# Convolution, attention and expert kernel: row maxima placed in 16 marked rows by one ScalarE copy, scores one head further ahead, steps of head, tail, ranks and taps reordered

## The chip, the cores and the metric

The kernel runs on one core of a Trainium2 chip. The metric is device time in microseconds (us); less is better. The engines are TensorE (PE; PEld is its weight load), VectorE (DVE), ScalarE (ACT), GpSimd (POOL) and SyncE (SP), each with its own instruction stream, tied together by semaphores.

## What is computed

```python
x = x + conv3x3(relu(norm(image_attention(conv3x3(x)))))   # 16 images, 128 channels, 16 x 16 pixels
t = tokens(x)                                              # 16 x 256 tokens of 128
z = layernorm(t)
sim = (z @ wq_s / 4) . (z @ wk_s)       # 8 heads of 16, within one image: 256 x 256 per head
retrieved = softmax(sim) @ (z @ wv_r)   # 2 value sets of 16
gate = softmax((z @ wq_r / 4) . (retrieved @ wk_ret))      # over the 2 sets
t = t + (gate . retrieved) @ w_out
z = layernorm(t)
t = t + sum over the best 2 of 8 experts: share * (silu(z @ W1[e]) @ W2[e])
```

## The kernel before

Three parts follow each other: the image attention with its convolutions (to about 142 us), the token stage (`token_attention`, to about 497), and the experts on rows scattered by expert (`experts`). The change is all in `token_attention`.

Tokens are in 8 chunks (g) of 512, two images each (b = 0, 1; image 2g + b); `body(g, ring, stage)` is one chunk on each engine, `last_body` the last. The stages are FIRST (g = 0), MIDDLE (1 to 5), LAST_BUT_ONE (6) and LAST (7). A body has two halves, one per image, of eight steps s, one per head. The order in each engine's stream is written out by hand; each engine works its own list in order, and a waiting instruction holds all that is behind it.

Per head, TensorE computes the scores of the *next* image (`scores`, L1596, banks ps_s), VectorE takes their row maxima (`row_max`, L1280). After eight heads VectorE negates and splits them into a high and a low part (`split_max`, L1289 to L1293), TensorE turns them (`turn_max`, L1605), and VectorE and ScalarE place two head pairs each into rows 96 to 99 of `q_stack` (`place_max`, L1298 and L1053). Rows 96 to 99 of `k_stack` hold ones and zeros that pick a head of a pair. So the second product, `shifted_scores` (L1617, 100 rows), gives transposed scores less their maximum. ScalarE takes the exponential (`exponent`, L1059), TensorE multiplies it with the values (`retrieve`, L1632, per pair of heads) and turns the result (`turn_ret`, L1641); ScalarE copies in between (`keep_pair`, `keep_ret`). TensorE's shifted scores of an image wait for `max_placed`.

Beside these run the other chunks' parts. *Head* of chunk g + 2: nine convolution taps (`conv_taps`, in MIDDLE stages by LATE_TAPS and behind step 7), `add_conv` on VectorE, `head_turn`, `keep_t` on ScalarE (L1024), `norm_stats` on VectorE (L1248 to L1256), `rstd` on GpSimd (a pow, L937), `normalise` on VectorE (L1262), `head_turn_back`, `split_zt`, `low_zt`, then `head_k`, and in the next body `head_q` and `head_tokens`. k and q of a chunk go to DRAM and come back stacked by head (SyncE's `stack`: `bounce` L890, `fill_k` L899, `fill_q` L905). *Tail* of chunk g - 1: `retrieve` parts 0 to 2 on VectorE (sum of a product of L1313, a gate whose exponential is ScalarE's L1083, o_tok L1334), `tail_turn` (L1655), `tail_out`, `add_attention`, statistics, `rstd`, `normalise_t2` on VectorE, `copy_rows` on GpSimd (L963), `tail_turn_back`, `tail_route`. *Ranks* of chunk g - 2: `route` parts 0 to 2 on VectorE, `share_exp` on ScalarE, `rank` on TensorE, `place` on VectorE, and GpSimd's `scatter` (eight indirect DMAs, L973).

Banks: ps_conv holds taps, z_tok's turn, k, and the tail's routing; ps_x holds the maxima's turn in most stages, t_chunk's turn, q, o_tok and the ranks; tokens use both.

## Time and profile before

| | us |
|---|---|
| runs | 684.0, 685.08, 688.95 |
| median | 685.08 |
| profiled execution, its own time | 685.38 |
| span of the profiled execution | 683.6 |
| TensorE busy in the span | 566.0 |
| VectorE busy | 475.9 |
| ScalarE busy | 333.1 |
| GpSimd busy | 262.6 |

The span runs from the first to the last instruction on the core. Busy times are sums over the whole span; what an edit in one stage is worth is read from the waits and the order of that stage.

### The profile page before, as it was taken

How to read it: one execution, taken by the hardware profiler on the slowest of the kernel's cores; microseconds unless marked ns; L12 is line 12 of the kernel's file. 1: busy time of each engine (PE TensorE's matmuls, PEld its weight loads, DVE VectorE, ACT ScalarE, POOL GpSimd, SP SyncE). 2: the span in 40 equal slices, each digit the busy share in tenths (PEclk: the TensorE clock that was granted, in tenths of full speed). 3: DMA queues.
4: the chain of work that ended last, by engine and by line, in shares of the span. 5: the costliest groups of instructions: out<-in, count | busy, mean ns of one | idle time of the engine just before them, and what ended most of it. 6: DMA issues, size and time to landing. Idle time of an engine off the chain costs nothing. (4 is left out here: it accounts for less than half of the span.)

```text
span 683.6 us, 10705 instructions
## 1 busy us (share of the span) xinstructions
PE 566.0 (83%) x3180; PEld 439.7 (64%) x3180; DVE 475.9 (70%) x1227; ACT 333.1 (49%) x718; POOL 262.6 (38%) x328
## 2 busy tenths in 40 slices
PE   5999999849788988979898887876169999999910
PEld 4888888636565767666666665654058888888810
DVE  6886774855557777777878778785537767767715
ACT  3322302233356465554636355544148888888800
POOL 3245443458000100141413314247603666666660
PEclk9999999959879999999999999998569999999965
DMA  7994145649531405041230505001278777776109
GB/s 262 365 347 145 57 170 185 203 164 372 153 116 39 155 1 155 1 151 36 96 92 31 157 3 184 9 25 48 76 251 293 234 243 230 246 235 221 51 6 363
DMA packets 55224, 105.46 MB, mean 154 GB/s; under 512 B 8744, under 2 KB 21689, under 8 KB 55040
## 3 DMA queue, kind: packets, MB, share of 16 engines
q1 hardware_dynamic: 50176, 96.24, 42.6%
q0 software_dynamic: 4992, 8.54, 3.6%
q8 instruction: 26, 0.43, 0.3%
q14 instruction: 30, 0.25, 0.1%
HBM read 58.15 MB, written 48.42 MB: 156 GB/s over the span
## 5 line engine op out<-in xcount | busy, mean ns | idle before, releaser
L1949 POOL DMA_INDIRECT y_slots<-virt,pad_l x92 | 95.7, 1041 | 72.5 <-DVE virt L2001 49.5
L1280 DVE TENSOR_REDUCE s_max<-bank 128x2 f32<-128x512 f32 x128 | 87.4, 689 | 40.3 <-PE bank L1596 39.8
L1059 ACT ACTIVATE s_expd<-bank 128x512 f32<-128x512 f32 x128 | 76.9, 602 | 53.5 <-PE bank L1617 52.3
L973 POOL DMA_INDIRECT x_slots<-rows,slot_of x64 | 63.1, 986 | 55.9 <-DVE rows L1408 38.3
L937 POOL TENSOR_TENSOR ln_rstd<-ln_var,power 128x4 f32<-128x4 f32 x17 | 17.4, 1026 | 173.4 <-DVE ln_var L1256 173.4
L1989 DVE TENSOR_TENSOR k_stack<-virt,k_stack 128x512 fp32r<-128x512 f32 x92 | 63.4, 689 | 24.9 <-ACT k_stack L1968 24.2
L1632 PE MATMUL bank<-s_expd,rvx 128*64 128x256 f32 x512 | 70.5, 397 | 1.5 <-ACT s_expd L1059 1.0
L61 PE MATMUL bank<-pad_h,u_h 128*128 128x512 f32 x144 | 59.9, 416 | 8.4 <-DVE pad_l L399 8.4
L1617 PE MATMUL bank<-q_stack,k_stack 100*128 100x256 f32 x256 | 61.8, 325 | 5.0 <-DVE q_stack L1298 5.0
L1968 ACT ACTIVATE k_stack<-virt 128x512 fp32r<-128x512 f32 x92 | 58.2, 633 | 10.1 <-PE bank L63 7.2
L1963 ACT ACTIVATE virt<-bank 128x512 f32<-128x512 f32 x92 | 55.0, 597 | 14.3 <-PE bank L63 13.9
L1596 PE MATMUL bank<-k_stack,q_stack 96*128 96x256 f32 x256 | 55.5, 303 | 3.9 <-DMA q_stack<-qk_rows 2.3
L63 PE MATMUL bank<-pad_h,u_l 128*128 128x512 f32 x144 | 58.0, 403 | 0.0
L62 PE MATMUL bank<-pad_l,u_h 128*128 128x512 f32 x144 | 57.9, 402 | 0.0
L1617 PEld LDWEIGHTS bank<-q_stack,k_stack 100*128 100x128 f32 x256 | 43.0, 199 | 18.0 <-DVE q_stack L1298 7.0
L1596 PEld LDWEIGHTS bank<-k_stack,q_stack 96*128 96x128 f32 x256 | 42.5, 204 | 6.2 <-DVE s_max L1280 2.8
L1632 PEld LDWEIGHTS bank<-s_expd,rvx 128*64 128x64 f32 x512 | 31.5, 138 | 22.6 <-ACT s_expd L1059 5.1
L1066 ACT ACTIVATE ret_f<-bank 128x256 f32<-128x256 f32 x64 | 24.4, 382 | 39.8 <-PE bank L1632 39.8
L61 PE MATMUL bank<-k_stack,pad_h 128*128 128x512 f32 x92 | 40.5, 440 | 0.0
L1984 DVE TENSOR_TENSOR k_stack<-bank,k_stack 128x512 fp32r<-128x512 f32 x23 | 15.9, 692 | 30.5 <-ACT k_stack L1958 30.5
L61 PEld LDWEIGHTS bank<-pad_h,u_h 128*128 128x128 f32 x144 | 27.8, 193 | 14.3 <-issue 8.3
L62 PE MATMUL bank<-k_stack,pad_h 128*128 128x512 f32 x92 | 36.7, 399 | 0.0
(260 smaller groups left out, 1321.8 us busy)
## 6 DMA issues: line engine op xcount, KB each, us to landing
x_slots<-blank SPq DMA_DIRECT2D x8, 2112.0 KB, 17.3
pad_h<-w_split SPq DMA_DIRECT2D x23, 512.0 KB, 4.4
q_stack<-w_split SPq DMA_DIRECT2D x23, 512.0 KB, 5.7
qk_rows<-qk SPq DMA_DIRECT2D x16, 512.0 KB, 3.0
k_stack<-qk_rows SPq DMA_DIRECT2D x96, 64.0 KB, 2.4
q_stack<-qk_rows SPq DMA_DIRECT2D x48, 128.0 KB, 2.6
pad_l<-x_slots SPq DMA_DIRECT2D x23, 264.0 KB, 5.2
e_raw<-in_w SPq DMA_DIRECT2D x16, 256.0 KB, 3.0
```

The lines of the kernel that those rows point to most:

```text
L61: pe.matmul(out, w_h, x_h, start=start, stop=False)
L62: pe.matmul(out, w_h, x_l, start=False, stop=False)
L63: return pe.matmul(out, w_l, x_h, start=False, stop=stop)
L973: pool.indirect_dma_start(out=x_slots[:, :], out_offset=bass.IndirectOffsetOnAxis(ap=slot_of[:, ring, k, j:j + 1], axis=0), in_=rows[:, ri ...
L1059: nc.scalar.activation(expd[:, s % 4].rearrange("p a i -> p (a i)"), ps_st[s % 2][:, :], ACT.Exp).then_inc(exp_done, 1)
L1280: nc.vector.tensor_reduce(s_max[:, :, s], ps_s[s % 2][:, :].rearrange("p (a j) -> p a j", a=2), AX.X, ALU.max).then_inc(max_done, 1)
L1596: last = pe.matmul(ps_s[s % 2][:, i * PIX:(i + 1) * PIX], q_stack[0:96, ring, s // 2, at + i * P:at + (i + 1) * P], k_stack[0:96, ring, s, ...
L1617: last = pe.matmul(ps_st[s % 2][:, i * PIX:(i + 1) * PIX], k_stack[0:100, ring, s, at + i * P:at + (i + 1) * P], q_stack[0:100, ring, s // ...
L1632: last = pe.matmul(ps_pv[p % 2][h * RF:(h + 1) * RF, 0:PIX], rvx[:, ring, 2 * b + a, :], expd[:, 2 * (p % 2) + h, a, :], start=(a == 0), s ...
L1949: pool.indirect_dma_start(out=y_slots[:, :], out_offset=bass.IndirectOffsetOnAxis(ap=ids, axis=0), in_=y_rows[:, t % 2, j, :], in_offset=N ...
L1968: nc.scalar.activation(hid_h[:, f], hid[:, f], ACT.Copy).then_inc(hid_high, 1)
L1989: nc.vector.tensor_tensor(hid_l[:, f], hid[:, f], f32(hid_h[:, f]), ALU.subtract).then_inc(hid_ready, 1)
```

## The change

Each image's maxima go to 16 rows (96 to 111) of all pairs of `q_stack` by one ScalarE copy that reads the turned maxima four times; the same 16 rows of `k_stack` mark, per head, its two rows with ones (`mark_heads`, two GpSimd copies in place of 24 memsets). VectorE's `place_max` is gone. Shifted scores use 112 rows. The turned maxima stay in one of the two score banks, no more in ps_x or ps_conv. `ahead_of` moves scores and row maxima one head on: at step s those of head s + 1 of the next image, at step 7 head 0 of the one after. `turn_max` stands at step 7. `head_q` of chunk g + 2 is issued at the end of body g (in FIRST also the old one at step 0). Tokens go to step 2, the tail's output to 6, its turn back to 5, its routing to 6, ranks to step 0 of the second half in ps_conv, the head's turn back to 5, taps to 3, 5, 6 and 7. The tail's normalise of chunks 0 to 5 moves from VectorE to GpSimd (`tail_rows`), its statistics to the second half, and VectorE's statistics wait for z_ready of the norm before (L1251's place). At the start four banks serve the first image's scores, `fill_q` of chunk 0 goes over ScalarE's DMA queue, and the low parts of images 12 to 15 come later. Lines left out are shown as "..."; where the lines of before are left out, they stand in the kernel above.

```diff
-    LATE_TAPS = {4: range(0, 2), 5: range(2, 3), 6: range(3, 4), 7: range(4, 6)}
+    LATE_TAPS = {3: range(0, 2), 5: range(2, 5), 6: range(5, 6), 7: range(6, 8)}
...
     def route_bank(u):
-        return ps_s[1] if u == IMAGE_A else ps_conv
-    def max_bank(stage):
-        return ps_x if stage in (FIRST, MIDDLE) else ps_conv
+        return ps_s[1] if u == IMAGE_A else ps_x if u < NCH - 2 else ps_conv
...
+    def ahead_of(image, s):
+        image, s = image + 1 + (s + LEAD) // S, (s + LEAD) % S
+        return (image, s) if image < 2 * NCH else None
+    def score_bank(image, s):
+        return ps_s[(9 * image + s - (1 if s else 2)) % 2]
+    def max_bank(image):
+        return ps_s[9 * image % 2]
+    first_banks = ps_s + ps_st
...
+        def first_stack():
+            sp.wait_ge(k_ready, 1)
+            bounce(sp, 0, 0, k_bounced)
+            sp.wait_ge(k_bounced, 16)
+            fill_k(sp, 0, 0, 0)
+            fill_k(sp, 0, 0, 1)
...
-        pool.memset(f32(m_split[:, :, :, :]), 0.0).then_inc(stack_init, 1)
+        pool.tensor_tensor(head_of[:, :], ident[0:2 * S, 0:2 * S:2], ident[0:2 * S, 1:2 * S:2], ALU.add
+                           ).then_inc(heads_marked, 1)
...
+        def normalise(n, dst, g):
+            pool.wait_ge(ln_power, n + 1)
+            for j in range(G):
+                last = pool.tensor_scalar(dst[:, j, :], chunk(resid, g)[:, j * P:(j + 1) * P], ln_mv[:, j, 0:1],
+                                          ln_rstd[:, j:j + 1], ALU.subtract, ALU.mult)
+            last.then_inc(z_ready, 1)
+        def tail_rows(g, ring):
+            rstd(tail_norm(g))
+            need(pool, scattered[ring], 2 * G * 16 * (g // 2))
+            normalise(tail_norm(g), rows[:, ring, 0, :, 0:P], g)
+        def mark_heads(ring):
+            pool.tensor_copy(k_stack[MAX_AT:MAX_AT + 2 * S, ring, :, :],
+                             head_of[:, :].unsqueeze(2).broadcast_to([2 * S, S, CH])).then_inc(ones_made, 1)
+        pool.wait_ge(stack_init, 2 * S)
+        pool.wait_ge(heads_marked, 1)
+        mark_heads(0)
+        pool.wait_ge(ones_made, 1)
         rstd(0)
         pool.wait_ge(ln_power, 1)
-        for part in range(1, 2 * S, 2):
-            pool.memset(ones_rows[0:2, part], 0.0).then_inc(ones_made, 1)
-        pool.wait_ge(ones_made, 3 * S)
+        mark_heads(1)
+        pool.wait_ge(ones_made, 2)
...
-            rstd(tail_norm(g - 1))
+            if g < NCH - 1:
+                tail_rows(g - 1, (g - 1) % 2)
+            else:
+                rstd(tail_norm(g - 1))
...
-        def place_max(g, b, ring, src=ps_x):
-            act.wait_ge(m_turned, 2 * g + b + 1)
-            for p in (2, 3):
-                nc.scalar.activation(q_stack[96:100, ring, p, b * PIX:(b + 1) * PIX],
-                                     src[32 * p:32 * p + 4, 0:PIX], ACT.Copy).then_inc(m_odd, 1)
+        def place_max(image):
+            act.wait_ge(m_turned, image + 1)
+            at = image % 2 * PIX
+            wide = max_bank(image)[0:2 * S, 0:PIX].unsqueeze(1).broadcast_to([2 * S, NP, PIX])
+            nc.scalar.activation(q_stack[MAX_AT:MAX_AT + 2 * S, image // 2 % 2, :, at:at + PIX], wide, ACT.Copy
+                                 ).then_inc(m_placed, 1)
...
+                if s == 0 and stage != LAST:
+                    split_k(g + 1)
+                if s == 1 and stage != LAST:
+                    split_q(g + 1)
+                if s == 2 and stage != LAST:
+                    keep_tok(g + 1, 0, 1 - ring)
+                    keep_tok(g + 1, 1, 1 - ring)
+                if s == 2 and stage != FIRST:
+                    gate(g - 1, 1)
+                if s == 5 and stage != FIRST:
+                    keep_o(g - 1)
+            place_max(2 * g + 1)
             keep_pair(g, 0, NP - 1)
...
             for s in range(S):
                 exponent(g, 1, s)
                 if s == 0:
                     keep_ret(g, 0, NP - 1)
                 pairs_behind(g, 1, s)
...
+                if s == 0 and stage in (FIRST, MIDDLE):
                     keep_t(g + 2)
...
+                if s == 0 and g >= 2:
+                    share_exp(g - 2)
+                if s == 3:
                     gate(g, 0)
...
+                if s == 5 and stage != FIRST:
+                    keep_z2(g - 1)
+                if s == 5 and stage in (FIRST, MIDDLE):
                     split_zt(g + 2)
+                if s == 7 and stage != FIRST:
+                    keep_logits(g - 1, 1 - ring)
+            place_max(2 * g + 2)
             keep_pair(g, 1, NP - 1)
...
                     gate(g - 1, 1)
...
+                if s == 5:
                     keep_o(g - 1)
                 if s == 6:
                     share_exp(g - 2)
+            place_max(2 * g + 1)
             keep_pair(g, 0, NP - 1)
...
+        def bounce_first_q():
+            act.wait_ge(q_ready, 1)
+            bounce(act, 0, 2, q_bounced)
+        def stack_first_q():
+            act.wait_ge(q_bounced, 16)
+            act.wait_ge(stack_init, 2 * S)
+            fill_q(act, 0, 0, 0)
+            fill_q(act, 0, 0, 1)
         keep_t(0)
         split_zt(0)
         keep_t(1, ps_s[1])
         split_k(0)
         split_q(0)
         keep_tok(0, 0, 0)
+        bounce_first_q()
         keep_tok(0, 1, 0)
+        split_zt(1)
+        stack_first_q()
         image_pair(6)
...
             dve.wait_ge(ln_steps, LS * n + 1)
+            need(dve, z_ready, n)
             nc.vector.memset(ln_var[:, :], 0.0)
...
-        def row_max(g, b, s):
-            dve.wait_ge(s_done, 2 * S * g + S * b + s + 1)
...
+                                    ).then_inc(max_done, 1)
+            if s == S - 1:
+                split_max(image)
+        def row_max_ahead(image, s):
+            if at := ahead_of(image, s):
+                row_max(*at, score_bank(*at))
+        def split_max(image):
...
         def body(g, ring, stage):
             for s in range(S):
...
+                row_max_ahead(2 * g, s)
+                if s == 0 and stage != LAST:
+                    low_k(g + 1)
+                if s == 0 and stage != LAST:
+                    low_q(g + 1)
+                if s == 1 and stage != FIRST:
+                    retrieve(g - 1, 1, 0)
+                if s == 2 and stage != FIRST:
+                    retrieve(g - 1, 1, 1)
+                if s == 2 and stage == FIRST:
+                    low(12)
+                if s == 3 and stage != FIRST:
+                    retrieve(g - 1, 1, 2)
+                if s == 3 and g >= 2:
+                    route(g - 2, ring, 0)
+                if s == 3 and stage == FIRST:
+                    low(13)
+                if s == 4 and stage == FIRST:
+                    low(14)
+                if s == 5 and g >= 2:
+                    route(g - 2, ring, 1)
+                if s == 5 and stage == FIRST:
+                    low(15)
+                if s == 6 and g >= 2:
+                    route(g - 2, ring, 2)
+                if s == 6 and stage != FIRST:
+                    add_attention(g - 1)
             for s in range(S):
...
+                if s == 0 and stage == MIDDLE:
                     add_conv(g + 2)
...
+                row_max_ahead(2 * g + 1, s)
+                if s == 0 and stage != FIRST:
+                    norm_stats(tail_norm(g - 1), t2_kept, g - 1)
                 if s == 1:
                     retrieve(g, 0, 0)
+                if s == 2 and g >= 2:
+                    place(g - 2, ring, ps_conv)
+                if s == 2 and stage in (FIRST, MIDDLE):
+                    norm_stats(2 * g + 2, t_kept, g + 2)
+                if s == 4 and stage in (FIRST, MIDDLE):
+                    normalise(2 * g + 2, z_tok, g + 2)
                 if s == 4:
                     retrieve(g, 0, 1)
                 if s == 5:
                     retrieve(g, 0, 2)
...
+                if s == 7 and stage in (FIRST, MIDDLE):
+                    low_zt(g + 2)
         def last_body():
             g, ring = NCH - 1, 1
             for s in range(S):
...
+                row_max_ahead(2 * g, s)
                 if s in (1, 2, 3):
                     retrieve(g - 1, 1, s - 1)
...
+                if s in (4, 5, 6):
+                    route(g - 2, ring, s - 4)
+            add_attention(g - 1)
+            norm_stats(tail_norm(g - 1), t2_kept, g - 1)
+            place(g - 2, ring, ps_conv)
             normalise_t2(g - 1, 0)
...
         normalise(1, z_tok, 1)
...
         low_zt(1)
...
+        add_conv(2, ps_pv[0])
         for s in range(S):
...
+            row_max(0, s, first_banks[s % 4])
+        for s in range(LEAD):
+            row_max(1, s, score_bank(1, s))
...
-                if dst is ps_conv:
-                    need(pe, tok_copied, 4 * g)
...
+        def scores(image, s, bank):
+            g, b = image // 2, image % 2
             if s == 0:
                 pe.wait_ge(stacked[b], STACK * (g + 1))
...
             at = b * PIX
             for i in range(2):
...
+                last = pe.matmul(bank[:, i * PIX:(i + 1) * PIX],
+                                 q_stack[0:96, g % 2, s // 2, at + i * P:at + (i + 1) * P],
+                                 k_stack[0:96, g % 2, s, at:at + PIX], start=True, stop=True)
             last.then_inc(s_done, 1)
...
+        def scores_in_turn(image, s):
+            if s == 0:
+                pe.wait_ge(max_done, S * image - 1)
+            elif s == 2:
+                pe.wait_ge(m_placed, image)
+            else:
+                pe.wait_ge(max_done, S * image + max(s - 1, 1))
+            scores(image, s, score_bank(image, s))
+        def scores_ahead(image, s):
+            if at := ahead_of(image, s):
+                scores_in_turn(*at)
+        def turn_max(image):
+            pe.wait_ge(m_steps, 3 * image + 3)
             for i in range(2):
...
+                src = f32(m_split[:, i].rearrange("p s c -> p (s c)"))
+                last = pe.transpose(max_bank(image)[0:2 * S, i * P:(i + 1) * P], src, ident[:, :])
             last.then_inc(m_turned, 1)
...
-                                 k_stack[0:100, ring, s, at + i * P:at + (i + 1) * P],
-                                 q_stack[0:100, ring, s // 2, at:at + PIX], start=True, stop=True)
+                                 k_stack[0:112, ring, s, at + i * P:at + (i + 1) * P],
+                                 q_stack[0:112, ring, s // 2, at:at + PIX], start=True, stop=True)
...
             max_placed(2 * g)
             for s in range(S):
                 shifted_scores(g, 0, s, ring)
...
+                scores_ahead(2 * g, s)
                 pairs_behind(g, 0, s, ring)
...
+                if s == 7:
+                    turn_max(2 * g + 1)
+                if stage == FIRST and s == 0:
+                    head_q(g + 1)
+                if s == 2 and stage != LAST:
+                    head_tokens(g + 1)
+                if s == 4 and stage != FIRST:
+                    need(pe, tok_copied, 4 * g + 6)
+                    tail_turn(g - 1)
+                if s == 6 and stage != FIRST:
+                    tail_out(g - 1)
                 if stage == MIDDLE and s in LATE_TAPS:
+                    if 0 in LATE_TAPS[s]:
+                        need(pe, tok_copied, 4 * g + 8)
                     conv_taps(g + 2, LATE_TAPS[s])
+            if stage == MIDDLE:
+                conv_taps(g + 2, range(8, 9))
             retrieve(g, 0, NP - 1, ring)
...
             max_placed(2 * g + 1)
             for s in range(S):
                 shifted_scores(g, 1, s, ring)
...
+                scores_ahead(2 * g + 1, s)
                 pairs_behind(g, 1, s, ring)
...
+                if s == 7:
+                    turn_max(2 * g + 2)
+                if s == 0 and g >= 2:
+                    if ahead:
+                        need(pe, t_ready, g + 3)
+                    else:
+                        need(pe, tok_copied, 4 * g + 8)
+                    rank(g - 2, ps_conv)
+                if s == 1 and ahead:
+                    need(pe, t2_kept, g + 0)
                     head_turn(g + 2)
...
+                if s == 5 and stage != FIRST:
+                    if ahead:
+                        need(pe, t_kept, g + 3)
+                    else:
+                        need(pe, t2_kept, g + 0)
+                    tail_turn_back(g - 1, 1 - ring)
+                if s == 5 and ahead:
+                    need(pe, spot_read, 4 * g - 7)
                     head_turn_back(g + 2, 2 * g + 3)
...
+                if s == 6 and stage != FIRST:
+                    tail_route(g - 1)
             retrieve(g, 1, NP - 1, ring)
...
             if ahead:
+                need(pe, zt_steps, 2 * g + 5)
                 head_k(g + 2)
+            if ahead:
+                need(pe, logits_kept, g + 0)
+                head_q(g + 2)
         def last_body():
             g, ring = NCH - 1, 1
             max_placed(2 * g)
             for s in range(S):
                 shifted_scores(g, 0, s, ring)
...
+                scores_ahead(2 * g, s)
                 pairs_behind(g, 0, s, ring)
...
+                if s == S - 1:
+                    turn_max(2 * g + 1)
+                if s == 5:
                     tail_turn(g - 1)
...
+                if s == 6:
                     tail_out(g - 1)
+                if s == 7:
+                    pe.wait_ge(logits_kept, g - 1)
+                    rank(g - 2, ps_conv)
             retrieve(g, 0, NP - 1, ring)
...
-        conv_taps(2, range(4, 8), ps_pv[0])
+        conv_taps(2, range(4, 9), ps_pv[0])
         head_k(1)
         for s in range(S):
-            scores(0, 0, s, 0)
-            if s == 0:
-                conv_taps(2, range(8, 9), ps_pv[0])
-        turn_max(0, 0)
-        pe.wait_ge(ones_made, 3 * S)
+            need(pe, max_done, s - 3)
+            scores(0, s, first_banks[s % 4])
+        scores_in_turn(1, 0)
+        turn_max(0)
+        pe.wait_ge(ones_made, 2)
```

## Rows read from the trace of the kernel before

**Rows 1.** The page, part 1: busy us (share) xinstructions

```profile
PE 566.0 (83%) x3180; PEld 439.7 (64%) x3180; DVE 475.9 (70%) x1227; ACT 333.1 (49%) x718; POOL 262.6 (38%) x328
```

**Rows 2.** Windows, chunk 4's halves: length, busy by engine, PEclk, DMA share, GB/s

```profile
317.60:333.67 16.07, 13.56 (x103) 9.83 (x102) 13.26 (x44) 9.71 (x25) 2.26 (x2) 1.00 0.01 2
333.67:355.57 21.90, 20.07 (x125) 15.13 (x125) 16.54 (x54) 9.99 (x26) 8.63 (x11) 1.00 0.48 145
```

**Rows 3.** Waits of PE, 190 to 458: us in total, times, longest

```profile
PE bank L1605 <- DVE m_split L1293: 12.3, 10, 1.6
PE bank L1655 <- DVE o_tok L1334: 11.7, 7, 1.9
PE bank L1617 <- DVE q_stack L1298: 5.0, 5, 1.2
PE bank L1557 <- DVE t_chunk L1242: 3.4, 5, 0.7
```

**Rows 4.** Timeline of PE, 328 to 345: start, us, what, [idle before <- releaser]

```profile
329.56 1.08 PE L1632 MATMUL bank<-s_expd,rvx 128*64 128x256 f32 x8
332.26 0.41 PE L1605 MATMUL bank<-ident,m_split 128*128 128x128 f32 x2 [1.62 <-DVE m_split L1293]
...
333.67 0.50 PE L1617 MATMUL bank<-q_stack,k_stack 100*128 100x256 f32 x2
334.01 0.40 PE L1596 MATMUL bank<-k_stack,q_stack 96*128 96x256 f32 x2
...
342.68 0.63 PE L1655 MATMUL bank<-ident,o_tok 128*128 128x128 f32 x4 [1.83 <-DVE o_tok L1334]
```

**Rows 5.** Timelines of DVE, 317 to 334 and 333 to 356

```profile
323.50 0.86 DVE L1248 BATCH_NORM_STATS2 ln_stats<-resid 128x6 f32<-128x128 f32 x4
...
324.89 0.68 DVE L1280 TENSOR_REDUCE s_max<-bank 128x2 f32<-128x512 f32 x1
...
331.73 0.18 DVE L1291 CAST m_split<-s_neg 128x16 fp32r<-128x16 f32 x1
...
332.75 0.87 DVE L1298 CAST q_stack<-bank 4x256 fp32r<-4x256 f32 x2
...
351.10 1.11 DVE L1262 TENSOR_SCALAR rows<-resid,ln_mv,ln_rstd 128x128 f32<-128x128 f32 x4 [0.15 <-POOL ln_rstd L937]
...
352.33 0.59 DVE L1291 CAST m_split<-s_neg 128x16 fp32r<-128x16 f32 x1
```

**Rows 6.** Timeline of ACT, 317 to 334

```profile
321.83 0.38 ACT L1066 ACTIVATE ret_f<-bank 128x256 f32<-128x256 f32 x1 [0.66 <-PE bank L1632]
...
322.70 0.60 ACT L1059 ACTIVATE s_expd<-bank 128x512 f32<-128x512 f32 x1
...
324.89 0.20 ACT L1105 ACTIVATE gap_e<-gap 128x4 f32<-128x4 f32 x1
```

**Rows 7.** Timelines of POOL, 95 to 142 and 350 to 382

```profile
132.61 0.90 POOL L289 TENSOR_SCALAR list_add<-tile_rows_f,row_f 2x23 f32<-2x23 f32 x1
...
349.95 1.04 POOL L937 TENSOR_TENSOR ln_rstd<-ln_var,power 128x4 f32<-128x4 f32 x1 [7.45 <-DVE ln_var L1256]
352.28 0.61 POOL L963 COPY rows<-rows 128x512 f32<-128x512 f32 x1 [1.29 <-DVE rows L1262]
```

**Rows 8.** The start: a window; PE's and DVE's timelines, 177 to 195

```profile
181.40:195.00 13.60, 10.06 (x32) 7.74 (x33) 8.51 (x16) 1.95 (x5) 0.00 (x0) 0.51 0.18 45
...
181.41 0.60 PE L1596 MATMUL bank<-k_stack,q_stack 96*128 96x256 f32 x2 [2.34 <-DMA q_stack<-qk_rows]
...
182.05 0.69 DVE L1280 TENSOR_REDUCE s_max<-bank 128x2 f32<-128x512 f32 x1 [2.65 <-PE bank L1596]
...
188.12 1.29 DVE L1280 TENSOR_REDUCE s_max<-bank 128x2 f32<-128x512 f32 x2 [0.29 <-PE bank L1596]
```

**Rows 9.** SP's timeline, 333 to 356; DMA view, 333 to 350 (KB, us to landing)

```profile
342.35 1.34 SPq L905 DMA_DIRECT2D q_stack<-qk_rows x3
...
q_stack<-qk_rows SPq DMA_DIRECT2D x6, 128.0 KB, 2.7
```

234 lines of the change are left out of this document (40 added, 194 removed).

## The prediction

> **What bounds the kernel now.** I read the page first, then the windows by half chunk, then TensorE's waits, then the timelines of one middle chunk. The page [rows 1] shows TensorE as the busiest engine, 83% against VectorE's 70%. The windows [rows 2] show one middle chunk (g = 4) in its two halves, 21.90 and 16.07 us, together 37.97 us. TensorE is busy for 20.07 + 13.56 = 33.6 us of it, at the full clock (1.00), VectorE for 16.54 + 13.26 = 29.8 us. So TensorE is the bound wherever it is fed, and about 4.2 us per chunk are waits. The waits view of the token stage [rows 3] names them: 12.3 us in which it waited to turn the maxima (`turn_max`), 5.0 us for these maxima to be placed, 11.7 us for `o_tok` at `tail_turn`, 3.4 us for `t_chunk` at `head_turn`. Together 32.4 us. In the timeline [rows 4] each wait stands in a middle chunk: 1.62 us ahead of the maxima and 1.83 us ahead of `tail_turn`; the head's 0.7 us is the third. After the last chunk GpSimd's scatters and then the experts follow; nothing there is edited, so I let that part move as a block: what the stage gains up to the first shifted scores of the last image, the end gains.
>
> **The change part by part.** I go by the profiled execution, 685.38 us around a span of 683.6; the median of the three runs, 685.08, is 0.3 lower.
>
> *The maxima's turn and placing.* Now the scores run one head further ahead. So the last row maximum and the split come at step 6, and `turn_max` stands at step 7 behind the pair's retrieve, the tail's products, shifted scores, scores and a turn. The retrieve's 1.08 and three starts of up to 0.34 [rows 4] alone are 2.1 us of TensorE work, against a need of one row maximum, 0.69, and the split's three short steps, 0.5 to 0.9 [rows 5]: covered, if VectorE is in time. Placing was two copies on VectorE (0.87, [rows 5]) beside two on ScalarE. Now it is one ScalarE copy of 1024 columns on 16 rows. No row shows that form. Bounds: 0.60 us for 512 columns, below; four copies of 256 columns at 0.38 = 1.53, above [rows 6]. The two forms differ by 256 columns and 0.22 us, so 1024 columns come to 0.60 + 2 x 0.22 = 1.04, which I take. It lies behind one retrieve (1.0), and in middle chunks behind taps or the k and q products as well. So all 17.3 us (12.3 + 5.0) go, and what is left is at the four turns without taps or head products behind them (first chunk, both of the last but one, last): 0.35 of copy that sticks out, and 0.3 where VectorE is late: 4 x 0.65 = 2.6 back.
>
> *The tail's turn.* VectorE gets the first ranks (1.1 us of `route`) behind the third part of `retrieve` instead of ahead, and TensorE puts two taps (1.5 us) ahead of `tail_turn`. Against it, tokens (keep_tok, 1.2 us on ScalarE) now stand ahead of the gate's exponential, on which VectorE waits. Followed step by step from the first shifted scores at T = 0: low_q ends at 3.5, tokens end at 4.6, the gate at 5.5, `o_tok` at 8.1, and TensorE arrives at 8.35. The 11.7 us go. In the last two chunks, which have no taps, the turn of the last is at step 5 and also late enough; in the last but one part may stay (inside the range).
>
> *The head's turn.* The 3.4 us go, since t_chunk is made first in the half. But keep_t and share_exp now stand ahead of exponential 1 on ScalarE, and keep_t waits for `head_turn`: 0.60 + 0.20 + 0.60 + signals 0.1 = 1.5 us from its end until the retrieve may start [rows 6], of which shifted scores and scores of step 2 cover 0.65. New wait 0.85 in six chunks, 5.1.
>
> *VectorE in the second half.* It loses placing (0.87) and gains the tail's statistics (1.4, [rows 5]): 13.26 - 0.87 + 1.4 = 13.8 us. TensorE's half without its waits and with head_q in it is 16.07 - 1.62 - 0.68 + 0.73 = 14.5. Only 0.7 us of slack in a half with three fixed meetings (scores 6, z_tok's turn, turn_max). Place and the statistics in one step make VectorE late by about 1 us at scores 6: I take 0.8 in each of four chunks and 0.4 in two, 4.0.
>
> *The tail's normalise on GpSimd.* Four tensor_scalars (1.11 on VectorE) go to GpSimd, behind its pow of 1.04. No row shows this form there. Bounds: 0.28 us each (VectorE's own, 1.11 / 4 [rows 5]) to 0.90 (GpSimd's only one with an operand per partition, of 23 columns [rows 7]), and beyond if its 105 more columns cost what the copy's 512 in 0.61 do (0.13): 1.03. I take 0.4 each, near to the copy's whole 0.61 for all the rows plus four starts, 1.6 in all. Queued behind it on GpSimd are copy_rows, the head's pow and the scatter; VectorE's next statistics wait for it (z_ready), and for these the head's z_tok. At U = 0 for the half's start the tail's statistics end at 2.8, pow at 3.9, normalise at 5.5, and the wait comes at 6.9. Covered up to 3.0 us for the four. What stays is the contention: [rows 5] shows the same cast of 16 columns at 0.18 and at 0.59 us, the long one at 352.33, when GpSimd's copy [rows 7] runs from 352.28 to 352.89. A VectorE operation was held until GpSimd was done. I take 0.4 in each of five chunks, 2.0. The Trainium skill (GPSIMD Engine Reference, Key points) says that GpSimd shares its SBUF interfaces with VectorE and contends with VectorE's two-port modes and two-input operations; by that rule the trace agrees, and the products of `retrieve`, two-input operations, may be held as well, which is the rival below.
>
> *Data a head earlier.* `stack` fills q for the next chunk at T = 8.7 to 10.0 (342.35 to 343.69 for T = 333.67), and a transfer lands 2.7 us later [rows 9]: T = 12.7. Scores of that image's head 0 are now asked for at step 7. In middle chunks that is about T = 15, covered. In the last but one, which has no taps, step 7 comes at about 11.4 and q at 12.7; in the first at about 11.9. Costs 1.3 + 0.8 = 2.1, with `turn_max` queued behind.
>
> *The start.* q's first fill goes over ScalarE's queue, beside k's. TensorE waited 2.34 us for q [rows 8]; then the stretch to 195 ran at a granted clock of 0.51, the level of 1.2 GHz. The tap inside the score loop goes ahead of it, t_chunk too, and four banks let TensorE run ahead, so VectorE does its eight maxima back to back. Before, they lasted from 182.05 to 189.41 [rows 8]; eight starts 0.61 apart and a last 0.69 take 5.0, 2.4 less. The longer copy takes 0.2 back: 2.2. Bounds: 0, and 5.2 if the clock keeps the upper level because TensorE idles less (some 3 us of the 13.6). GpSimd's 25 small memsets become two copies of 4096 columns: 0.61 x 8 = 4.9 each by the copy's row, about the time of what they replace, beside taps; worth 0.
>
> Matrix products with 112 rows in place of 100 stream the same columns: 0.
>
> **The sum.** Gone: 32.4 + 2.2 = 34.6. New: 2.6 + 5.1 + 4.0 + 2.0 + 2.1 = 15.8. Net 18.8. The profiled run would be 685.4 - 18.8 = 666.6, by the median 666.3: 666.
>
> **The rivals.**
> (a) *TensorE nearly without waits.* The order by hand was made engine by engine, and my followed schedules may meet waits that a loop that has settled doesn't show. For it: 32.4 us are real idle time of the busiest engine. Half the new waits (7.9) and the clock kept at the start (3): 685.4 - 34.6 + 7.9 - 3 = 656.
> (b) *GpSimd's normalise ends too late.* Each at the 0.90 of [rows 7] with 0.13 more for columns is 1.03, four are 4.1: z_ready at U = 8.0, 1.1 late for the head's statistics, then pow and z_tok, so `head_turn_back` is 1.2 us later in five chunks: 666 + 6 = 672. For it: the only row with such an operand. Against it: that row is one instruction, of 23 columns, and the first of its kind.
> (c) *VectorE becomes the bound.* Its 0.7 us of slack in the second half isn't enough for the order of its steps, and each middle chunk gives back 3.8 us, nearly its whole gain, instead of 0.8: 666 + 5 x 3.0 = 681, no clear change. For it: 13.8 of 14.5. Against it: its first half has slack (16.54 - 1.4 - 1.11 - 0.87 = 13.2 of TensorE's 20.07 - 0.73 = 19.3).
> (d) *Slower: VectorE held by GpSimd.* Place: the second half, where GpSimd's four operations run beside retrieve, place and the statistics. Price: VectorE stands still for each whole operation, as in the cast's row, 4 x 1.03 = 4.1, and (b)'s 1.2 on top, in six chunks: 32 us, of which 2 are in the sum: 666 + 30 = 696. It decides from 20.8 / 6 = 3.5 us per chunk on, that is 0.9 per operation with all of it held. Against it: the pow of 1.04 runs beside VectorE now, and VectorE's statistics and row maxima next to it keep their times.
> (e) That it doesn't do what it says: scores a head further ahead are only asked for earlier and wait for `max_done`. Same lag of two heads in two banks as before, so no gain from the banks; only the turn of the maxima gains. It is in the sum.
>
> **How the numbers follow.** Forecast 0.56, (a) 0.15, (b) 0.11, (c) 0.10, (d) 0.08. The forecast's own range is 659 to 673 (its five new terms at 0.5 to 1.4 times). The range over all is 655 to 681: it holds (a)'s and (c)'s centres and leaves out (d) and the far sides. A measurement of this kernel tells about 1% from no change, 678.2 and 691.9. Forecast, (a) and (b) lie below 678.2, with some of the forecast and (b) leaking over: 0.80 faster. (c) and what leaks: 0.12 same. (d): 0.08.
>
> **What would show it.** Right: in the waits of TensorE the groups of `turn_max`, placing and `tail_turn` under 1 us each per chunk, middle chunks at 34.8 to 35.8 us, the retrieve behind exponential 1 waiting 0.5 to 1, one wait for q's transfer in the last but one chunk, the placing copy near 1.04, GpSimd's tensor_scalar at 0.3 to 0.6. Wrong: that tensor_scalar near 1 us, VectorE's two-input operations stretched beside it, a wait of VectorE's statistics for GpSimd, TensorE waiting 3 us per half for row maxima, or the part behind the last image's first shifted scores growing.

## The result and the profile after

The changed kernel took 682.67 us (median of 20 runs, 677.61 to 690.6), the kernel before in the same rounds 686.52 (20 runs, 683.32 to 691.4). The ratio is 0.9926, 95% interval 0.9902 to 0.995: about 0.7% faster, which is within the 1% that the prediction called no change. It is taken over the runs in the usual, faster state alone (690.6 is left out), so it isn't the quotient of the two medians, 0.994. The forecast was 666, the range 655 to 681. The profiled execution took 677.61 us around a span of 675.8, 7.8 less than before's 683.6; it was the fastest of the 20.

The page of the changed kernel, part 1 (as [rows 1]), and its windows of chunk 4's two halves (as [rows 2]; here the first half stands first):

```profile
PE 567.4 (84%) x3180; PEld 441.6 (65%) x3180; DVE 460.2 (68%) x1171; ACT 339.6 (50%) x702; POOL 276.8 (41%) x330
```

```profile
333.05:352.91 19.86, 19.42 (x122) 14.43 (x120) 13.51 (x39) 9.88 (x24) 1.76 (x2) 1.00 0.46 144
352.91:370.31 17.40, 14.34 (x107) 10.71 (x106) 13.55 (x51) 10.67 (x25) 12.17 (x16) 1.00 0.06 20
```

The first half went from 21.90 to 19.86 us and is now nearly all TensorE work (19.42). The second went the wrong way, from 16.07 to 17.40 (the 16.07 in [rows 2] is the half just ahead, chunk 3's second; chunk 4's own took 16.04), with 14.34 of TensorE work: 3.06 us of waits. The waits of TensorE, 185 to 455 us (total, times, longest), beside [rows 3]:

```profile
PE bank L1635 <- DVE s_max L1331: 8.6, 7, 1.4
PE bank L1684 <- ACT s_expd L1099: 7.5, 14, 0.8
PE bank L1596 <- DVE z_tok L1313: 3.3, 4, 0.9
PE bank L1669 <- ACT q_stack L1093: 1.8, 4, 1.2
PE bank L1658 <- DVE m_split L1347: 1.6, 2, 1.2
PE bank L1707 <- DVE o_tok L1382: 0.9, 1, 0.9
```

All four groups of [rows 3] went nearly as forecast: 1.6 us are left at `turn_max` (L1658), 1.8 at placing, 0.9 at `tail_turn` (L1707), nothing at `head_turn`. In their place stand 8.6 us for row maxima ahead of the scores (L1635), 7.5 for the exponential at the retrieve (L1684) and 3.3 for the head's normalise (L1596, `z_tok`). TensorE's timeline has one of each in the second half of a middle chunk, and 0.79 + 1.36 + 0.91 = 3.06 is the whole gap of the window:

```profile
356.30 1.08 PE L1684 MATMUL bank<-s_expd,rvx 128*64 128x256 f32 x8 [0.79 <-ACT s_expd L1099]
361.59 0.51 PE L1635 MATMUL bank<-k_stack,q_stack 96*128 96x256 f32 x2 [1.36 <-DVE s_max L1331]
363.67 0.63 PE L1596 MATMUL bank<-ident,z_tok 128*128 128x128 f32 x4 [0.91 <-DVE z_tok L1313]
```

VectorE's timeline there shows why the last two come late. It waited 2.06 us for the last tap at the end of the first half (`t_chunk`), 1.00 us for the first scores of the second (the row maximum at 353.69), and then never until the head's normalise, except once, for GpSimd:

```profile
352.01 0.69 DVE L1292 TENSOR_TENSOR t_chunk<-bank,resid 128x512 f32<-128x512 f32 x1 [2.06 <-PE bank L63]
...
354.30 0.86 DVE L1298 BATCH_NORM_STATS2 ln_stats<-resid 128x6 f32<-128x128 f32 x4
...
359.04 0.86 DVE L1298 BATCH_NORM_STATS2 ln_stats<-resid 128x6 f32<-128x128 f32 x4
360.36 0.06 DVE L1302 MEMSET ln_var<- 128x4 f32 x1 [0.46 <-POOL rows L966]
...
360.86 1.28 DVE L1331 TENSOR_REDUCE s_max<-bank 128x2 f32<-128x512 f32 x2
362.18 1.34 DVE L1313 TENSOR_SCALAR z_tok<-resid,ln_mv,ln_rstd 128x128 f32<-128x128 f32 x4
```

The first statistics (354.30 to 355.8) are the tail's, new in this half; the second are the head's. GpSimd's timeline of the stretch:

```profile
355.87 1.04 POOL L960 TENSOR_TENSOR ln_rstd<-ln_var,power 128x4 f32<-128x4 f32 x1 [20.75 <-DVE ln_var L1307]
357.09 3.14 POOL L966 TENSOR_SCALAR rows<-resid,ln_mv,ln_rstd 128x128 f32<-128x128 f32 x4 [0.18 <-POOL ln_rstd L960]
```

From first shifted scores to first shifted scores, the difference of the two profiled executions adds up like this:

| stretch | before | after | difference |
|---|---|---|---|
| to the first shifted scores | 191.95 | 192.47 | +0.5 |
| first chunk | 28.45 | 28.73 | +0.3 |
| first halves of the five middle chunks | 109.65 | 99.29 | -10.4 |
| their second halves | 79.45 | 87.02 | +7.6 |
| from there to the last image | 48.42 | 41.75 | -6.7 |
| from the last image's first shifted scores to the end of the span | 225.68 | 226.54 | +0.9 |

The first row holds two things. VectorE's last step ahead of the token stage, which no edit touches, came 1.7 us earlier in the changed kernel's execution (the first line is of the kernel before, the second of the changed one):

```profile
147.04 0.23 DVE L695 TENSOR_SCALAR norm_b<-mean_sum,gb 128x16 f32<-128x16 f32 x1
```

```profile
145.34 0.23 DVE L695 TENSOR_SCALAR norm_b<-mean_sum,gb 128x16 f32<-128x16 f32 x1
```

From there to the first shifted scores it is 44.91 us before and 47.13 after: the start itself got 2.2 us longer, and 1.7 us of the profile's 7.8 are luck.

### The profile page after: what moved, and what is told of

The parts are those of the page before. It is cut to its first block and busy times, and to the rows that moved or that the text cites. A ratio compares the mean times of both kernels' runs of the same rounds, so it can differ in the third digit from the quotient of the medians.

```text
span 675.8 us, 10656 instructions
## 1 busy us (share of the span) xinstructions
PE 567.4 (84%) x3180; PEld 441.6 (65%) x3180; DVE 460.2 (68%) x1171; ACT 339.6 (50%) x702; POOL 276.8 (41%) x330
## 3 DMA queue, kind: packets, MB, share of 16 engines
HBM read 58.15 MB, written 48.42 MB: 158 GB/s over the span
## 5 line engine op out<-in xcount | busy, mean ns | idle before, releaser
L1684 PE MATMUL bank<-s_expd,rvx 128*64 128x256 f32 x512 | 71.0, 399 | 7.5 <-ACT s_expd L1099 7.5
L1008 POOL DMA_INDIRECT x_slots<-rows,slot_of x64 | 62.7, 980 | 18.6 <-issue 18.1
L1635 PE MATMUL bank<-k_stack,q_stack 96*128 96x256 f32 x256 | 55.4, 305 | 11.1 <-DVE s_max L1331 8.6
L1669 PE MATMUL bank<-q_stack,k_stack 112*128 112x256 f32 x256 | 61.8, 325 | 1.8 <-ACT q_stack L1093 1.8
L1669 PEld LDWEIGHTS bank<-q_stack,k_stack 112*128 112x128 f32 x256 | 42.0, 197 | 16.8 <-issue 10.5
L1635 PEld LDWEIGHTS bank<-k_stack,q_stack 96*128 96x128 f32 x256 | 41.5, 202 | 14.4 <-DVE s_max L1331 10.6
L1684 PEld LDWEIGHTS bank<-s_expd,rvx 128*64 128x64 f32 x512 | 31.5, 138 | 29.4 <-ACT s_expd L1099 12.6
L61 PE MATMUL bank<-k_stack,pad_h 128*128 128x512 f32 x92 | 40.8, 443 | 0.0
L62 PE MATMUL bank<-k_stack,pad_h 128*128 128x512 f32 x92 | 37.0, 402 | 0.0
L63 PE MATMUL bank<-k_stack,pad_h 128*128 128x512 f32 x92 | 36.7, 399 | 0.0
## 6 DMA issues: line engine op xcount, KB each, us to landing
x_slots<-blank SPq DMA_DIRECT2D x8, 2112.0 KB, 17.2
```

Of the source, the lines that this page charges most:

```text
L61: pe.matmul(out, w_h, x_h, start=start, stop=False)
L62: pe.matmul(out, w_h, x_l, start=False, stop=False)
L63: return pe.matmul(out, w_l, x_h, start=False, stop=stop)
L1008: pool.indirect_dma_start(out=x_slots[:, :], out_offset=bass.IndirectOffsetOnAxis(ap=slot_of[:, ring, k, j:j + 1], axis=0), in_=rows[:, ri ...
L1635: last = pe.matmul(bank[:, i * PIX:(i + 1) * PIX], q_stack[0:96, g % 2, s // 2, at + i * P:at + (i + 1) * P], k_stack[0:96, g % 2, s, at:a ...
L1669: last = pe.matmul(ps_st[s % 2][:, i * PIX:(i + 1) * PIX], k_stack[0:112, ring, s, at + i * P:at + (i + 1) * P], q_stack[0:112, ring, s // ...
```

## The experiments

My theory after the result: what moved into the second half on VectorE, the tail's statistics above all, eats what the first half gained; and the marking copies hold VectorE at the start. Rivals: GpSimd's slow normalise, or keep_t ahead of the exponential. Each ratio is to the kernel before, with its 95% interval. Lengths of halves are read between first shifted scores. "From `norm_b`" is the time from VectorE's L695 to the first shifted scores; it leaves out what varies ahead of the stage. For comparison, the changed kernel: first shifted scores at 192.47, 47.13 from `norm_b`, the last three middle second halves 17.35, 17.40 and 17.34.

**Both marking copies ahead of the first power.**

```diff
         mark_heads(0)
-        pool.wait_ge(ones_made, 1)
-        rstd(0)
-        pool.wait_ge(ln_power, 1)
         mark_heads(1)
         pool.wait_ge(ones_made, 2)
+        rstd(0)
         rstd(1)
```

> Changed kernel with both mark_heads copies ahead of the first rstd on GpSimd. Theory (the second marking copy, 3.6 us on GpSimd from 163.96, holds VectorE's first normalise, which took 4.47 us in place of 1.77): the first normalise takes 1.1 to 1.2 us, the first shifted scores start about 2.7 us earlier (189.8 for 192.5), all later stages the same length, span about 2.7 us shorter. Rival (the long normalise has another cause, e.g. the pointer operands read while their bank is written): it stays above 3 us and nothing moves. If the marking costs GpSimd so long that rstd(0) is late, half of the gain goes.

681.35 us, ratio 0.9929 (0.99 to 0.9959). A miss on the start: first shifted scores at 193.59, 48.06 from `norm_b`. The first normalise took its 1.11 us, but the hold only moved. VectorE's timeline of the changed kernel:

```profile
154.10 4.80 DVE L1268 TENSOR_TENSOR pad_l<-virt,pad_h 128x256 fp32r<-128x256 f32 x4 [0.35 <-ACT pad_h L1044]
...
163.93 4.47 DVE L1313 TENSOR_SCALAR z_tok<-resid,ln_mv,ln_rstd 128x128 f32<-128x128 f32 x4 [1.24 <-POOL ln_rstd L960]
```

and of this one, with GpSimd's line behind it:

```profile
154.29 8.23 DVE L1266 TENSOR_TENSOR pad_l<-virt,pad_h 128x256 fp32r<-128x256 f32 x4 [0.33 <-ACT pad_h L1042]
...
167.75 1.11 DVE L1311 TENSOR_SCALAR z_tok<-resid,ln_mv,ln_rstd 128x128 f32<-128x128 f32 x4 [1.24 <-POOL ln_rstd L960]
```

```profile
154.23 7.34 POOL L977 CAST k_stack<-head_of 16x4096 fp32r<-16x4096 f32 x2
```

VectorE's four subtractions end just after the two copies (162.5 and 161.6). The copies hold whatever VectorE does beside them; a later experiment puts one where it has little to do.

**The tail's statistics at step 7 of the first half.**

```diff
                 if s == 6 and stage != FIRST:
                     add_attention(g - 1)
+                if s == 7 and stage != FIRST:
+                    norm_stats(tail_norm(g - 1), t2_kept, g - 1)
             for s in range(S):
...
-                if s == 0 and stage != FIRST:
-                    norm_stats(tail_norm(g - 1), t2_kept, g - 1)
```

> Changed kernel with the tail's statistics on VectorE at step 7 of the first half (where VectorE sat idle 2.06 us) in place of step 0 of the second. Theory (VectorE is the late engine in the second half only, because of the order): row maxima of head 4 come 1.4 us earlier and z_ready from GpSimd is there, so TensorE's waits for s_max (1.36 per chunk) and z_tok (0.9) fall to under 0.5 together; second halves of middle chunks go from 17.35 to 15.2 - 15.8, span 8 to 10 us shorter than the changed kernel. Rival (GpSimd's queue sets z_tok): the wait for s_max goes, the wait for z_tok takes over with 1.5 to 2, gain under 3 us.

668.9 us, ratio 0.9766 (0.9719 to 0.9813), span 666.9, second halves of 15.46 to 15.69 in the last four middle chunks. Windows of chunk 4, then the waits of TensorE, 190 to 445 us:

```profile
328.68:348.49 19.81, 19.37 (x123) 14.43 (x121) 14.79 (x49) 9.88 (x24) 3.07 (x4) 1.00 0.48 144
348.49:364.15 15.66, 14.10 (x107) 10.70 (x106) 12.13 (x41) 10.57 (x25) 10.82 (x15) 1.00 0.07 23
```

```profile
PE bank L1684 <- ACT s_expd L1099: 7.4, 14, 0.8
PE bank L1596 <- DVE z_tok L1313: 2.9, 4, 0.8
...
PE bank L1635 <- DVE s_max L1331: 1.2, 2, 1.0
```

VectorE has 1.4 us less in the second half (12.13 for 13.55), the half is 1.74 shorter, and the first half pays nothing for it: it had that idle time. The wait for row maxima falls from 8.6 to 1.2; the one for `z_tok` stays (2.9 for 3.3), which wasn't expected. GpSimd's normalise starts earlier too, so this run alone doesn't clear it; a later one does.

**keep_t and share_exp behind exponential 1.**

```diff
-                if s == 0 and stage in (FIRST, MIDDLE):
+                if s == 1 and stage in (FIRST, MIDDLE):
                     keep_t(g + 2)
-                if s == 0 and g >= 2:
+                if s == 1 and g >= 2:
                     share_exp(g - 2)
```

> Changed kernel with keep_t and share_exp on ScalarE at step 1 (behind exponential 1) in place of step 0. Theory: the retrieve's wait of 0.8 behind exponential 1 goes in six chunks. But in middle chunks VectorE's lateness at scores 6 is a fixed meeting that this doesn't move, so TensorE only arrives earlier and waits there: the wait for s_max grows from 1.36 to about 2.1, span 0 to 1.5 us shorter. Rival (waits add up): 4 to 5 us shorter.

690.52 us, ratio 1.0051 (1.0016 to 1.0086): half a per cent slower than before. The waits, 190 to 458:

```profile
PE bank L1635 <- DVE s_max L1331: 11.7, 12, 1.4
PE bank L1596 <- DVE z_tok L1313: 4.9, 6, 0.9
PE bank L1635 <- DMA q_stack<-qk_rows: 2.5, 1, 2.5
PE bank L1684 <- ACT s_expd L1099: 1.9, 6, 0.3
```

The wait for the exponential went from 7.5 to 1.9 us and came back at the row maxima and `z_tok`: two second halves took 17.36 and 17.39, as before the edit. Three others took 18.58, 21.44 and 21.65, at a granted clock of 0.91, 0.76 and 0.76. Windows through the last of these:

```profile
360.86:365.00 4.14, 4.14 (x38) 3.43 (x36) 3.25 (x15) 3.37 (x9) 1.04 (x1) 1.00 0.00 0
365.00:370.00 5.00, 3.05 (x22) 1.96 (x20) 4.40 (x21) 2.29 (x6) 4.89 (x8) 1.00 0.00 0
370.00:374.00 4.00, 3.08 (x19) 2.46 (x19) 3.78 (x12) 2.10 (x5) 3.20 (x4) 0.59 0.12 37
374.00:378.00 4.00, 4.00 (x20) 3.05 (x17) 0.85 (x4) 0.94 (x4) 2.90 (x4) 0.50 0.16 52
```

TensorE was busy for 3.05 of 5.00 us, and for 3.08 of the next 4.00, in which the clock fell; then it stood at 0.50, the level of 1.2 GHz, though TensorE was busy again without a gap. These three halves cost 9.6 us over 17.37 each, and 688.1 - 9.6 = 678.5; of the 2.7 us that this still is above the changed kernel's 675.8, 2.35 are in the very first half (17.16 against 14.81), with a wait of 2.5 us for q's transfer. The profile is no odd one out: all ten runs had a mean granted clock of 0.904 to 0.919, nineteen of the changed kernel's twenty one of 0.920 to 0.930.

**All three edits.**

> The three edits of e1, e2 and e3 together in the changed kernel. Theory: they add, since each removes what covers the other: 2.7 from the start, 8 to 10 from the statistics, 4 to 5 from keep_t, which now counts: middle chunks 34.3 to 35 us for 37.25, span 14 to 17 us below the changed kernel's, ratio to before 0.968 to 0.975. Rival (GpSimd's 3.14 us of normalise with copy_rows and rstd behind it bind the half): chunks at 36 or more, no more than 8 us.

669.59 us, ratio 0.9769 (0.9734 to 0.9803), span 666.7. A miss: no better than the statistics alone. The last four middle second halves stay at 15.47 to 15.69. keep_t's gain doesn't add to the statistics', and the marking copies moved forward bring nothing here either: first shifted scores at 194.31, 47.97 from `norm_b`, 0.8 longer than in the changed kernel (0.9 in the first experiment).

**The tail's normalise back on VectorE, nothing else.**

```diff
-            if g < NCH - 1:
-                tail_rows(g - 1, (g - 1) % 2)
-            else:
-                rstd(tail_norm(g - 1))
+            rstd(tail_norm(g - 1))
...
                 if s == 1:
                     retrieve(g, 0, 0)
+                if s == 1 and stage != FIRST:
+                    normalise_t2(g - 1, 1 - ring)
```

> The changed kernel with the tail's normalise back on VectorE (step 1 of the second half), so GpSimd keeps only the power. Its four operations there took 3.14 us against some 1.1 us on VectorE. Theory (the second half is set by how much VectorE has to do ahead of the row maxima and of the head's normalise; the tail's statistics, 1.4 us, are what moved into it): VectorE gets 1.1 us more and is freed of the 0.46 us wait for GpSimd's last operation, so the second halves stay within 17.0 to 17.9 us, the span within 675 to 680. Rival (GpSimd's slow normalise is the cause, by its length and by what it takes from VectorE): second halves of 16.0 to 16.5 us, a span of 669 to 672.

683.12 us, ratio 0.993 (0.9893 to 0.9967); undisturbed second halves 17.61 to 17.64, against 17.35. The span, 681.6, is above the expected range; of its 5.8 us over the changed kernel's, 2.4 stand in the first chunk (the transfer of q again) and 2.5 in a half near the end at a clock of 0.89, which the edit doesn't touch. So GpSimd's 3.14 us were not what made the half long, in spite of each operation taking 0.79 instead of my 0.4: taking the 1.11 off VectorE was slightly good.

**Statistics and keep_t, marking copies left alone.**

> The changed kernel with the tail's statistics at step 7 of the first half and keep_t behind exponential 1 (step 1). Where the statistics alone stand there, PE still waits 0.5 us at step 2 of each half (7.4 us in 14) for an exponential that keep_t holds. If that wait was on the path, the second halves go from 15.6 to 15.0 and the span from 666.9 to some 663; if the head's normalise (power on GpSimd, then behind two row maxima on VectorE) sets the half anyway, as the run of all three edits suggests (15.7), they stay at 15.5 to 15.7 and the span at 665 to 667, and no half falls to the lower clock.

670.9 us, ratio 0.9739 (0.968 to 0.9798), span 669.8; the last four middle second halves 15.48 to 15.69, the same as without keep_t. The second reading holds: the wait at the retrieve is real and worth nothing there. From 190 to 457 us it fell from 7.4 to 2.8 us in all, while the one for row maxima rose from 1.2 to 3.9 and the one for `z_tok` from 2.9 to 4.3. Of the 2.9 us more of span 2.2 stand before the first shifted scores (194.69 against 192.49), where nothing differs between the two kernels: the start alone varies by that much from one execution to another.

**Statistics in the first half, second marking copy behind both first normalises.**

```diff
         pool.wait_ge(ln_power, 1)
+        rstd(1)
+        pool.wait_ge(z_ready, 2)
         mark_heads(1)
         pool.wait_ge(ones_made, 2)
-        rstd(1)
```

> The statistics at step 7 of the first half, and the second marking copy of GpSimd (3.6 us) behind both start normalises instead of between the two powers. If a marking copy holds VectorE only while it works on the same memory, the first normalise takes 1.11 instead of 4.47 us, and the first shifted scores start at 189 to 190 instead of 192.5, the span is 663 to 664.5. If the copy holds whatever VectorE does next again (the low part of zt of the second chunk), 0.6 to 2 us of that come back: 190 to 191.5, span 664.5 to 666. Rival (the start is bound by the transfer of q and not by the normalise): first shifted scores at 192 to 193.

664.75 us, ratio 0.9656 (0.9595 to 0.9716), span 663.0. First shifted scores at 188.56, 3.9 earlier than with the statistics alone. In all five profiles with the second copy in its old place they stood between 192.4 and 194.7, in the three with it here between 188.5 and 189.6: at least 2.8 us of it are more than the start varies. From `norm_b` it is 47.0 to 48.8 us against 42.3 to 43.2, at least 3.8 us less, and now shorter than before's 44.91 (44.20 in the one other profile with before's start, that of the next experiment). VectorE's timeline, then GpSimd's:

```profile
163.69 1.11 DVE L1314 TENSOR_SCALAR z_tok<-resid,ln_mv,ln_rstd 128x128 f32<-128x128 f32 x4 [1.24 <-POOL ln_rstd L960]
...
174.63 1.25 DVE L1320 TENSOR_TENSOR zt_l<-zt,zt_h 128x512 fp32r<-128x512 f32 x1 [2.96 <-ACT zt_h L1069]
```

```profile
171.74 3.60 POOL L977 CAST k_stack<-head_of 16x4096 fp32r<-16x4096 f32 x1 [1.64 <-DVE z_tok L1314]
```

The copy now meets only one subtraction, which takes 1.25 instead of 0.69 and ends 0.5 us after the copy.

**The kernel before, with the choice one step later.**

```diff
-                if g >= 2 and s in (2, 3, 4):
-                    route(g - 2, ring, s - 2)
+                if g >= 2 and s in (3, 4, 5):
+                    route(g - 2, ring, s - 3)
```

> The kernel BEFORE the change with only the choice's three parts on VectorE one step later in the first half (3, 4, 5 instead of 2, 3, 4), so that the row maxima and the retrieval of the earlier steps go ahead of them. PE's wait at the tail's turn (11.7 us in all, 1.83 us in each) is for VectorE's last retrieval. If that wait goes by the order on VectorE alone, the first halves lose 0.7 to 1.2 us each and the span 4 to 7 (683.6 to 677 to 680). Rival (what VectorE does later holds the row maxima and the split instead): the wait moves to the turn of the maxima, span within 1.5 of 683.6.

684.01 us, ratio 0.9943 (0.9903 to 0.9982). The wait at the tail's turn fell from 11.7 to 6.0 us, first halves at full clock from 21.85 to 20.71. The wait for the turn of the maxima hardly moved (12.0 for 12.3), and the middle second halves at full clock kept their 15.26 and 16.04. But three others took 16.33 to 16.59 at a clock of 0.95 to 0.97, two first halves 21.44 and 21.76 at 0.96 and 0.94, and the last but one chunk's first half 18.28 at 0.94, for 17.49 at 1.00 before; the very first half took 1.3 us more (clock 0.80 for 0.88). From the first shifted scores of all to the last it is 265.1 us against 266.0. Neither expectation held as written: the wait does go by VectorE's order, half of it went, and most of that was lost again, here to the granted clock and not to other waits.

**On top of that: head's statistics ahead of placing the choice, its normalise at step 3; then keep_t too.**

```diff
+                if s == 2 and stage in (FIRST, MIDDLE):
+                    norm_stats(2 * g + 2, t_kept, g + 2)
                 if s == 2 and g >= 2:
                     place(g - 2, ring, ps_conv)
-                if s == 2 and stage in (FIRST, MIDDLE):
-                    norm_stats(2 * g + 2, t_kept, g + 2)
-                if s == 4 and stage in (FIRST, MIDDLE):
+                if s == 3 and stage in (FIRST, MIDDLE):
                     normalise(2 * g + 2, z_tok, g + 2)
```

"That" is the kernel with the statistics and the late marking copy.

> The statistics of the tail in the first half and the late marking copy as before, and in the second half the head's statistics ahead of the placing of the choice (1.0 us) on VectorE and its normalise at step 3 instead of 4. PE waits 0.8 us for that normalise in each second half. Theory: the second half is set by the chain from the head's statistics to the normalise; it starts 1.0 us earlier and its last part stands ahead of a row maximum: second halves of 15.0 to 15.3 instead of 15.7, first shifted scores still at 188.5, span 660.5 to 662. Rival (the row maximum that it is put ahead of becomes late, PE waits for the row maxima of step 4 instead): second halves at 15.6 to 15.8, span 663.

664.27 us, ratio 0.9661 (0.9626 to 0.9695), span 662.8; second halves 15.23 to 15.25 in the last three middle chunks. The wait for `z_tok` is down to 0.2 us in all, `turn_max` has 0.28 in a chunk again: the half is 0.45 shorter, as the theory had it, and the five together 1.5. The span gained 0.2 only: 0.3 went at the start, 0.8 in the first chunk, 0.5 at the last image (14.22 against 13.74), which in part is how profiles vary.

> The same with keep_t and share_exp behind exponential 1 as well. In the kernel with all three edits keep_t brought nothing, which would be because the head's normalise ended last. If so, with that chain shortened keep_t's 0.5 us in each second half now count: second halves of 14.5 to 15.0, span 658 to 660.5. Rival (keep_t itself starts that chain: its later start, some 0.6 us, makes the statistics late by as much as the exponentials win): no gain over the kernel without it, 15.0 to 15.3 and within 0.7 us of its span.

663.92 us, ratio 0.9658 (0.9626 to 0.9691), span 662.0; second halves 15.24 and 15.25 again, so the rival's number holds. Its reason doesn't: in chunk 4's second half keep_t ran at 2.16 us into the half in both kernels, the head's statistics at 4.09 and 4.10, and the normalise ended at 8.09 and 8.10. VectorE's stream stayed where it was, and TensorE, which came earlier, waited for it. The waits of TensorE, 190 to 440:

```profile
PE bank L1636 <- DVE s_max L1332: 2.9, 5, 0.7
PE bank L1659 <- DVE m_split L1348: 2.9, 5, 1.2
PE bank L1685 <- ACT s_expd L1100: 2.7, 7, 0.8
```

A third time the 0.8 us of keep_t turn up elsewhere, now at the row maxima. The last three kernels can't be told apart by their times; all three beat both kernels, by 3.4% against before.

## Why the prediction was wrong

**Waits that go: right.** 32.4 us were said to go, with 2.6 coming back at the maxima; what stands there now is 1.6 + 0.3 + 1.8 + 0.9 = 4.6 (the 0.3 is a turn of the maxima that waits for ScalarE). ScalarE's placing copy took 1.01 us against 1.04. First halves came to 19.86 where the followed schedule gave 19.3; the sum's own bound, TensorE's work, is 19.42.

**VectorE in the second half: the step that failed.** I counted VectorE's load right (13.8 us; the window shows 13.55) and TensorE's (14.5; 14.34), called the difference 0.7 us of slack and charged 0.8 per chunk. TensorE's two waits for VectorE there came to 1.36 + 0.91 = 2.27 us, 1.47 more in each. The sum's terms for the half, 14.5 + 0.8 + 0.85 + 0.4 for the contention, make 16.55; it took 17.35, and one 17.86 at a clock of 0.90. The sum over an engine hid its order: VectorE stands idle at the border of the halves, 2.06 us for the last tap and 1.00 for the first scores, and the tail's statistics, whose input VectorE had written by 348.8, start only behind both and ahead of two things TensorE meets soon, the row maximum of scores 6 and `z_tok`. Moving these 1.4 us over the half's border, into VectorE's idle time, took 1.74 us off each half. Rival (c) named this place with 3.8 per chunk instead of 0.8; it was some 2.3, halfway between. Rival (a) is out: TensorE's waits of over 0.1 us still add up to 24.4.

**keep_t: size right, meaning wrong.** The forecast was 0.85 in six chunks, 5.1; the chunk shows 0.79. But the terms of the second half were added as if each were paid in full. They lie one behind another on the same path: in three pairs of kernels that differ by this edit alone, the undisturbed halves were equally long (17.35 and 17.36, 15.66 and 15.69, 15.25 and 15.25). What decides is when VectorE's results are there, and a wait of TensorE ahead of that is paid inside it.

**GpSimd's normalise: size wrong, effect small.** 0.79 us per operation (18.8 for 24), nearer to the 0.90 of [rows 7] than to my 0.4. VectorE waited 0.46 for the last of them. With the operations back on VectorE the half grew by 0.26. The contention of 2.0 us was not there in the middle: a row maximum beside the normalise took 0.68 us as elsewhere, and small operations up to 0.1 more. The head's own normalise did take 1.34 instead of 1.11, beside GpSimd's first scatter. Rival (d) is out, and (b) too: undoing its cause brought nothing.

**The start: wrong sign.** Maxima back to back went as forecast, in 4.88 us for eight; but the first shifted scores came at 192.47, 0.5 later than before and not 2.2 earlier; from `norm_b` the start got 2.2 longer, 4.4 off the forecast. I had costed the two marking copies at nothing, "beside taps", looking at TensorE. They took 3.60 us each, and VectorE stood still beside them: its first normalise took 4.47 us instead of 1.11. I had the mechanism in hand from the cast of 0.59 us, and applied it to the wrong operations of GpSimd. Moving one copy gave 3.8 us or more back, and with it there the start is 1.0 to 2.7 us shorter than in the two profiles with before's start, around the 2.2 forecast: the step that failed here is the zero for the copies. The Trainium skill (GPSIMD Engine Reference, section 8, Key points) says that the contention is with VectorE's two-port modes and two-input operations. The held subtractions have two SBUF inputs, so for them and the marking copies the trace agrees; the held normalise reads one, and no row shows its mode. For GpSimd's normalise of the middle chunks the trace shows next to nothing of it: a two-input product beside it (L1365) took 0.26 us against 0.17 without it.

**q's transfer a head earlier.** Forecast 2.1; the changed kernel's profile shows 0.2, but six of the nine kernels made from it 2.1 to 2.5 in one wait of the first chunk, whose first half then took 16.6 to 17.2 us instead of 14.5 to 14.9. So the size was right as an upper end, and it was one wait in the first chunk, where I had 0.8 there and 1.3 in the last but one. What decides whether it comes stays open.

**The median.** The profile's 7.8 us are 3.9 in the medians; the profiled execution was the fastest of the 20, and 1.7 us of it were gained ahead of the stage, where nothing is edited. The rest goes with the granted clock: the runs with a mean clock of 0.920 to 0.923 took 682.8 to 685.2 us, those with 0.927 to 0.930 took 677.6 to 682.6. In the changed kernel's profile one second half stood at 0.90, and a relative with the same waits (both marking copies first) had a half of 21.65 at 0.76. The six kernels whose second halves wait 1.6 us or less had every middle half at 1.00. They also spread over 2 to 4 us only, where the changed kernel spread over 13; but they had 4 to 6 runs against 20, and the relative spread over 4.1 in ten. That the 3 us of waits in a half let the clock fall fits the profiles; it wasn't tested by itself.

By the terms: the profile's 7.8 us are 11.0 short of 18.8. The start is 4.4 short. The middle second halves are some 5.6 short: about 7 for VectorE's term and 0.8 for the one at the lower clock, less the 2.0 for a contention that didn't come. The middle first halves are 2.4 short (2.1 each in place of 2.6). The part behind the last image's first shifted scores, which was to move as a block, grew by 0.9. Against that stand the 1.7 us of luck ahead of the stage, and some 0.6 in the chunks at both ends, where q's transfer cost next to nothing in this profile.

## What to carry to other kernels

Before summing an engine's load over a stretch, find where in it the engine stands idle and which of its results is met first: 1.4 us of statistics ahead of such a meeting cost about their length here, and moving them over the border of the half into idle time gave it back (from 0.7% to 2.3% faster than before). Don't add waits that follow one another on one path; remove the one that ends last and look again (here the next one stood 0.45 us behind). And an operation hidden from the bound engine is still beside someone: a long GpSimd copy within SBUF belongs where VectorE is idle.

## What was not expected of the hardware

A GpSimd copy of 16 partitions by 4096 elements (3.60 us) held VectorE's first normalise for 3.36 us, and two of them four subtractions for some 6.6 us (8.23 instead of about 1.6). The same engine's four normalising operations of 0.79 us, on 128 partitions, held VectorE's operations beside them by about 0.1 us. Why the one holds and the other doesn't stays open.

The granted clock can cost a whole optimisation: with a real 0.8 us wait taken away the kernel was slower than before, 690.5 us against the changed kernel's 682.7, with three halves of 18.6 to 21.7 us in place of 17.4 in its profile. Why it was this edit that brought the lower clock stays open.
